# Who adds the level terms in a state space stage: seven additions per sequence moved from POOL to VectorE

## What is computed

```python
cum = jnp.cumsum(a, axis=2)                       # a = dt * A
diff = cum[:, :, :, None, :] - cum[:, :, None, :, :]
Lmat = jnp.exp(jnp.where(tril, diff, -jnp.inf))
M = CB * Lmat * dtc[:, :, None, :, :]             # CB = C B^T, 128 x 128
Yd = jnp.einsum('bcijh,bcjhp->bcihp', M, xs_c)
y = (Yd + Yoff).reshape(Bsz, L, H, P) + D[None, None, :, None] * xs
yz = y * (z * jax.nn.sigmoid(z))
yn = yz * jax.lax.rsqrt(jnp.mean(yz * yz, axis=-1, keepdims=True) + EPS) * norm_w
return yn @ W_out.T
```

## Time and profile before

| | |
|---|---|
| median of 3 runs | 2271.22 us (2270.86 to 2271.75) |
| the profiled execution | 2272.82 us, span 2270.9 us |
| busy: PE, DVE, ACT, POOL | 90%, 73%, 59%, 56% of the span |
| state space stage | from about 930 to 1360 us of the span |
| a full step (m = 5) | 26.6 us, from gating to gating |
| TensorE clock granted, mean | 0.975 |

### The profile page before, as it was taken

The page is one execution under the profiler, slowest core; times in us unless marked ns, Lnnn a source line. Parts: engine busy times, 40 slices in busy tenths (PEclk is TensorE's granted clock), DMA queues, the critical chain, the costliest instruction groups (busy, mean ns, idle before and its releaser), DMA issues.

```text
span 2270.9 us, 35496 instructions
## 1 busy us (share of the span) xinstructions
PE 2040.4 (90%) x10014; PEld 1337.3 (59%) x10116; DVE 1663.7 (73%) x3833; ACT 1332.0 (59%) x5022; POOL 1260.5 (56%) x1508
## 2 busy tenths in 40 slices
PE   7889999999999996888989976999999999999996
PEld 5546666566665664555555543666666666666664
DVE  8755666676666766678887764778888888877886
ACT  3655666666666564333333224777777777777773
POOL 0153444544444532566666662667777777776775
PEclk9999999999999998999999987999999999999998
DMA  5000000000000012000000002000000000000000
GB/s 216 1 20 3 3 4 2 5 2 2 2 2 5 0 47 73 26 19 19 19 19 10 1 2 80 3 4 6 6 8 5 6 5 6 5 5 8 3 3 8
DMA packets 30093, 37.61 MB, mean 17 GB/s; under 512 B 3328, under 2 KB 24320, under 8 KB 29312
## 3 DMA queue, kind: packets, MB, share of 16 engines
q1 hardware_dynamic: 29952, 36.11, 4.8%
HBM read 34.00 MB, written 2.10 MB: 16 GB/s over the span
## 4 chain that ended last, share of the span: by engine, by line
PE 66%; DVE 12%; ACT 11%; issue 7%; POOL 3%; DMA 1%; SPq 0%; DVEq 0%; POOLq 0%; ACTq 0%
PE xa_pJB L730 5%; PE xa_pS L749 5%; PE xa_pO L823 5%; PE fa_pJB L1837 5%; PE xa_pY L853 5%; PE ssm_pX L1328 5%; PE xa_pJA L730 4%; PE fa_pS L1856 4%; PE ssm_pL L1322 3%; PE fa_pY L1887 3%; PE fa_pO L1874 3%; PE fa_pJA L1817 3%; PE fa_pH L1938 2%; DVE ssm_y L1598 2%; PE fa_pJB L1817 2%
## 5 line engine op out<-in xcount | busy, mean ns | idle before, releaser
L1276 POOL TENSOR_TENSOR ssm_y<-ssm_y,ssm_term 128x512 f32<-128x512 f32 x112 | 142.0, 1268 | 127.6 <-DVE ssm_term L1544 125.4
L1773 POOL TENSOR_TENSOR fa_rs<-fa_rs,all_minus_half 128x4 f32<-128x4 f32 x192 | 198.3, 1033 | 15.0
L1964 ACT ACTIVATE fa_qT<-fa_pH,all_fa_head_vec 128x512 f32<-128x512 f32 x128 | 99.6, 778 | 171.8 <-PE fa_pH L1938 171.8
L1973 ACT ACTIVATE fa_pS<-fa_pS,fa_nb 128x128 f32<-128x128 f32 x512 | 183.1, 393 | 7.0 <-issue 6.6
L1770 POOL TENSOR_TENSOR fa_rs<-fa_ms,all_eps5w 128x4 f32<-128x4 f32 x192 | 44.1, 229 | 240.1 <-ACT fa_q_junk L1957 132.2
L1856 PEld LDWEIGHTS fa_pS<-fa_kT,fa_qT 128*128 128x128 f32 x1024 | 124.7, 192 | 65.4 <-ACT fa_qT L1964 58.5
L1796 POOL TENSOR_TENSOR fa_cat<-fa_ov,fa_om 128x512 bf16<-128x512 f32 x128 | 154.0, 1203 | 5.3
L681 POOL TENSOR_TENSOR xa_rs<-xa_ms,all_eps 128x4 f32<-128x4 f32 (+1 forms) x65 | 13.7, 211 | 257.8 <-ACT xa_junk L898 257.8
L1856 PE MATMUL fa_pS<-fa_kT,fa_qT 128*128 128x128 f32 x1024 | 149.0, 289 | 2.5 <-ACT fa_qT L1964 0.9
L1787 POOL TENSOR_TENSOR fa_ov<-fa_ob,fa_om 128x512 f32<-128x512 bf16 x128 | 148.0, 1156 | 4.6 <-DVE fa_om L2151 4.6
L749 PE MATMUL xa_pS<-all_shared_weights,xa_qT 128*128 128x256 f32 x512 | 126.5, 389 | 23.4 <-ACT all_shared_weights L929 17.5
(11 more groups left out here) (327 smaller groups left out, 5936.8 us busy)
## 6 DMA issues: line engine op xcount, KB each, us to landing
all_shared_weights<-in_fa_w SPq DMA_DIRECT2D x12, 512.0 KB, 3.8
fa_cat<-in_fa_wproj SPq DMA_DIRECT2D x8, 512.0 KB, 3.8
all_shared_weights<-in_xa_wq SPq DMA_DIRECT2D x1, 2048.0 KB, 13.8
xa_wo<-in_xa_wo SPq DMA_DIRECT2D x1, 2048.0 KB, 17.5
xa_ctxT<-in_ctxT SPq DMA_DIRECT2D x16, 128.0 KB, 2.1
all_shared_weights<-in_fa_wkvx SPq DMA_DIRECT2D x1, 2048.0 KB, 9.0
fa_ctxT<-in_ctxT SPq DMA_DIRECT2D x16, 128.0 KB, 2.1
out_x<-all_X SPq DMA_DIRECT2D x16, 128.0 KB, 1.7
```

The costliest lines, as they stand in the source:

```text
L1773: pool.tensor_tensor(rs[:, j % 2, cols], rs[:, j % 2, cols], env.mhalf[:, cols], ALU.pow)\
L1973: last = act.activation(four(pS[j % 2])[:, i, :], four(pS[j % 2])[:, i, :], ACT.Exp, bias=nb[:, j % 2, i:i + 1], accum_out=rsum[:, j % 2, ...
```

## The change

The block of seven additions is taken out of POOL's program. VectorE's `terms(*levels)` gets a second loop behind the first: after the terms of the call, it adds each to y, with the same tiles and semaphores. In `terms(0, 1)` and `terms(4, 5)` both additions stand behind both terms. Every addition waits for its term (`term_done`) and for the addition before it, or y0 (`y_added`, `y0_done`), both now VectorE's own. `pool_rms` and `norm.pool_rstd` stay on POOL, one behind the other.

```diff
         def steps(m, side, attend, front, back, first):
-            if attend:
-                for l in range(LEVELS):
-                    if l == 0:
-                        pool.wait_ge(s["y0_done"], now(m, 0))
-                    else:
-                        pool.wait_ge(y_added, now(m, 0, LEVELS, l - 1))
-                    pool.wait_ge(term_done, now(m, 0, LEVELS, l))
-                    pool.tensor_tensor(y[:, side, :], y[:, side, :], term[:, in_turn(side, l), :], ALU.add)\
-                        .then_inc(y_added, 1)
-                    if l == 1 and back:
-                        pool_rms(m - 1)
-                    if l == 6 and back:
-                        norm.pool_rstd(pool, m - 1, 0)
-            elif back:
+            if back:
                 pool_rms(m - 1)
                 norm.pool_rstd(pool, m - 1, 0)
...
                     dve.tensor_tensor(heads(term[:, in_turn(side, l), :]), heads(pL[in_turn(side, l)][:, :]),
                                       per_head(dec[:, side, l, :]), ALU.mult).then_inc(term_done, 1)
+                for l in levels if attend else ():
+                    dve.wait_ge(term_done, now(m, 0, LEVELS, l))
+                    if l == 0:
+                        dve.wait_ge(s["y0_done"], now(m, 0))
+                    else:
+                        dve.wait_ge(y_added, now(m, 0, LEVELS, l - 1))
+                    dve.tensor_tensor(y[:, side, :], y[:, side, :], term[:, in_turn(side, l), :], ALU.add)\
+                        .then_inc(y_added, 1)
```

## The result

| | before | after |
|---|---|---|
| median | 2271.3 us (2270.8 to 2271.8, 6 runs) | 2280.3 us (2279.3 to 2284.1, 6 runs) |
| profiled execution, its span | 2272.82, 2270.9 | 2280.51, 2278.7 |
| state space stage, from the gating of m = 2 to that of m = 17 | 387.5 | 394.7 |
| busy PE, DVE, ACT, POOL | 90, 73, 59, 56% | 90, 75, 58, 50% |
| TensorE clock granted, mean | 0.975 | 0.971 |

A forecast was written before the change was run, and what follows sets the result against it. Each step was taken as bound by TensorE, then ScalarE up to xd, then VectorE. Collisions of 2.7 (seven steps), 1.2 (five) and 0.8 (m = 12) gave +4.7 us, 2275.9 by the median; forecast 2273.6 to 2276.8, whole range 2271.0 to 2280.0.

The forecast's parts named there:

- What bounds the step: State space step: TensorE sets the time up to the sixth term, TensorE and ScalarE up to xd, VectorE behind it.
- T: Start of the sixth term (level 5) in a step of the state space stage; 1064.06 in m = 5.
- Points (3) and (4): (3) before the sixth term, +0.86 us on the fifth covered; (4) behind it, 1.31 more, xdt still done before the decays.
- full steps: Seven steps with both the weight chunk's low part and its mean (m = 2, 4 to 9); +0.38 us each.
- Point (5): Behind the sixth term, addition 6, POOL's skip and xdt collide: xd +0.15 or +0.38 us by order; 0.38 or 0.25 taken.
- light steps: Five steps with less VectorE work (m = 10, 11, 13, 14, 15); +0.25 us each.
- Point (6): Special steps: m = 12 +0.8 us as VectorE is already late; m = 1, m = 3 and the last step 0.
- second rival: Chance 0.16: longer gap before transposes drops TensorE's clock, 1.3 us in one to three more steps, 2277.2 to 2279.8.
- First rival: Chance 0.20: additions only fill VectorE's idle time and xd doesn't move; not slower, 2270.3 to 2271.2.
- Third rival: POOL's xd runs before VectorE's at step end: +0.7 us in nine steps, about 2282; 0.06, shared with VectorE late at T.

The follow-up runs named there:

- e3: Changed kernel with POOL's skip folded into VectorE's y0, all seven additions still on VectorE; 2269.3 us, ratio 0.9993.
- e5: Only additions 0 to 3 moved to VectorE, 4 to 6 left on POOL; 2279.7 us, ratio 1.0031.
- e14: Additions 0 to 3 on VectorE, 4 to 6 on POOL, unread TensorE products filling both gaps (gated y, transposed input); 2275.8 us, ratio 1.0013.
- e4: Changed kernel with unread TensorE products ahead of the wait for the gated y (m = 2 to 9, 13); 2274.7 us, ratio 1.0015.
- e6: Only additions 4 to 6 moved to VectorE, 0 to 3 left on POOL; 2278.7 us, ratio 1.0025.
- e8: Changed kernel with POOL's centring of the weight chunk put behind addition 3; 2261.0 us, ratio 0.9948.
- e15: Changed kernel with unread TensorE products ahead of the waits for the gated y and the transposed input; 2274.3 us, ratio 1.0010.
- e13: Kernel before with unread TensorE products ahead of the waits for the gated y and the transposed input; 2271.8 us, ratio 0.9999.
- e1: Kernel before plus an idle VectorE reduction of 128 columns ahead of xd; 2277.9 us, ratio 1.0030.
- e10: Kernel before with POOL's centring of the weight chunk put behind addition 3, skip left on POOL; 2261.4 us, ratio 0.9951.
- e2: Kernel before with POOL's skip folded into VectorE's y0; 2270.5 us, ratio 0.9998.
- e7: Kernel before with unread TensorE products ahead of the wait for the gated y (m = 2 to 9, 13); 2272.0 us, ratio 1.0007.
- e12: Additions 0 to 3 on VectorE, 4 to 6 on POOL, unread TensorE products ahead of the wait for the gated y; 2278.3 us, ratio 1.0025.

## Why the prediction was wrong

- **What bounds the step**, T set by TensorE, xd by ScalarE, the rest by VectorE: right. L1475 and L1477 at 0.22 us, the sixth term in time (but right behind the fifth, without the short wait that was forecast), the end of a step unchanged.
- **Points (3) and (4), the additions' own work covered up to T and behind it:** right in the full steps, and e3 confirms it for the whole kernel. Addition 0.60 to 0.71 each, as taken.
- **Point (5), the collision:** the mechanism was right, and the page "SBUF — State Buffer" of the Trainium skill, section "Who interferes with whom", which spoke against the change, is borne out: xdt ended 0.55 us behind skip's end (1070.93 for 1070.38), the 0.54 that y0 had shown. The size was off. Of the two orders it was addition 6 first, for which 0.15 stood there, while 0.38 was taken; it came to 0.25, since skip ended 0.08 later than worked out (18.86 us behind the gating for 13.22 + 5.56) and xdt and xd another 0.02. For the seven full steps the sum had 2.7; without the clock they gave 1.2, five times a quarter, since m = 6 had the loss already and m = 8 gave 0.29 back. The sum was read off m = 5 alone; the rows of m = 6 and 8 would have told. In m = 8 the stalls of point (3) were not hidden up to T. For the five light steps 1.2 was taken and 1.0 measured.
- **Point (6):** m = 12 cost 1.2 for 0.8. The fifth term came 1.00 us later against the gating (13.68 for 12.68) instead of 0.86, and here skip did go ahead of addition 6, which took 1.57 us, while xdt took 0.68. VectorE in m = 12, for the earlier trace rows:

```profile
1252.54 1.28 DVE L1531 TENSOR_TENSOR ssm_term<-ssm_pL,ssm_dec 128x512 f32<-128x512 f32 x2
...
1257.18 1.57 DVE L1539 TENSOR_TENSOR ssm_y<-ssm_y,ssm_term 128x512 f32<-128x512 f32 x1
1258.67 0.68 DVE L1585 TENSOR_TENSOR ssm_xdt<-ssm_xs,ssm_dt 128x512 f32<-128x512 f32 x1
```

m = 3 gave 0.5 back and the last step lost 0.33, where both were put at 0.
- Together the part without the clock is 3.3 us by the profile of the change, below the 4.7 of the forecast.
- **The step that failed is the second rival, the clock.** It had the mechanism, the gap, the place and the price (1.3 us in a step) but a chance of 0.16 and one to three steps, argued down with "1.89 us is not much shorter and is harmless". That sentence was the mistake. The harmless gap was today's 1.89; the sum itself made it 2.25. Behind small products at full clock the traces show no slow z product in the gaps of 1.81 to 1.90 us, a slow one in all four of 1.96 or 1.97 (three in e5, one in e14) and in ten of fourteen of 2.17 to 2.21, the four quick ones in the changed kernel, e4, e6 and e8. In the profiled execution the clock cost 3.9 us, half of the loss in the stage; e15 and e13 give 3.6 by the stages and 6.5 by the medians. It should have been in the sum. Three steps were this rival's own upper case, 2279.8, half a microsecond from the median, but that nearness is luck in part: its 4.7 without the clock is 1.4 above the 3.3 of the profile, while the medians lie 1.8 further apart than the stages.
- **First rival** (only idle time filled): false as the kernel stands, true as soon as skip is out of the way (e3). **Third rival** (POOL's xd ahead): not in the changed kernel, since both xd wait for the late xdt; e1 shows it, at 0.2 us a step and not 0.7.

## What to carry to other kernels

Moving work into idle time of another engine is not free when it then stands in front of an operation with two SBUF inputs that the first engine also wants to overlap: look at who is waiting when the moved work ends, and price the one that loses. Before costing a delay in tenths of a microsecond, look at how long TensorE stands idle ahead of the next large product; if one step of the same kernel with a slightly longer gap already ran at the lower clock, that term belongs in the sum. The gap itself was the better target: a wide POOL operation that made it could run elsewhere, and moving that gained 10.6 us in the kernel before (e10), more than the change lost.

## What the hardware showed that was not expected

- A gap of 1.89 us ahead of the transposes was never followed by a low clock in full steps. Behind small products at full clock one of 1.96 was every time (4 of 4), one of 2.17 to 2.21 in ten of fourteen (m = 8 of the changed kernel had a granted clock of 1.00), and one of 3.53 (e2, m = 13) was not. So the length of the gap alone does not decide; what else does is not shown. The price is 1.1 to 1.7 us on the z product, less what overlaps.
- Slow phases take turns: after a step whose small products ran at the low clock (5.42 us for 3.79) the next gap is 0 to 0.9 us in full steps and the z product is quick. Ahead of a gap of 1.9 us or more a low clock there is free, because TensorE would have waited anyway. Where the gap is short or filled it is paid: 25.72 for 25.25 us in e8, 27.44 for 26.60 in e7, and 25.71 for 24.97 in m = 15 of the kernel before. Filling the gaps up to m = 9 and in m = 13 of the kernel before (e13) removed all the slow products of its profiled stage and gained nothing measurable in the median (0.9990 to 1.0009).
- Which of two engines goes first can turn on 0.2 us (e1), and an operation of 3.35 us becomes one of 2.38 by it, while its rival goes from 2.34 to 3.94.

What stays open: why the first four additions alone cost as much in the median as all seven even with the gaps filled (e12, e14), when the profiled executions show less; why e1's median rises more than its stage; and what makes the stretches outside the stage differ by up to 6.6 us between single executions of the same programs.
